# Staging the per-tile score-bound pass and the attention-value matmuls inside the head loop of a sparse-offset attention stage

## What is computed

```python
src = jnp.clip(t_idx[:, None] - offsets[None, :], 0, None)
Kg = k[:, :, src, :]
Vg = v[:, :, src, :]
scores = jnp.einsum('bhnd,bhnod->bhno', q, Kg) * scale
scores = scores + pos_bias.T[None, :, None, :]
scores = jnp.where(invalid[None, None], -jnp.inf, scores)
alpha = jax.nn.softmax(scores, axis=-1)
out = jnp.einsum('bhno,bhnod->bhnd', alpha, Vg)
gate = jax.nn.sigmoid(xn @ w_gate + b_gate)
x = x + out * gate @ w_out
```

## Time and profile before

| | us |
|---|---|
| median of two runs | 5897.9 |
| the profiled execution | 5880.33 |
| its span, slowest of 8 cores | 5878.7 |
| spans of the eight cores | 5846.4 to 5878.7 |
| PE busy | 4105.7 (70%) |
| DVE busy | 974.8 (17%) |
| ACT busy | 573.7 (10%) |
| exp, line 608, 256 times | 262.1 |
| mask multiply, line 611, 256 times | 177.2 |

### The profile page before, as it was taken

One profiled execution on the slowest core, in us unless ns is written; L12 is line 12 of the kernel. 1 busy time (PEld: TensorE's weight loads), 2 busy tenths in 40 slices (PEclk: granted clock), 3 DMA queues, 4 the chain that ended last, 5 costly groups with the idle time before them and its releaser, 6 DMA issues.

```text
span 5878.7 us, 54400 instructions; the slowest of 8 cores (5846.4 to 5878.7 us)
## 1 busy us (share of the span) xinstructions
PE 4105.7 (70%) x21474; PEld 2041.9 (35%) x21778; DVE 974.8 (17%) x1764; ACT 573.7 (10%) x546; POOL 194.4 (3%) x159
## 2 busy tenths in 40 slices
PE   0111777244444444454877898999999898999999
PEld 0000323233333333321433343444444443444444
DVE  0344224122222222234011111000000020000001
ACT  0000010111111111100200020000000100000000
POOL 0000000000000000000000010000000010000000
PEclk9655889555555555556988999999999999999999
DMA  3322121100000000023022366655656656555657
GB/s 57 83 57 57 29 71 26 30 12 12 6 12 7 10 12 6 12 60 93 19 40 61 118 76 83 82 72 73 83 75 103 119 72 88 77 72 78 80 72 136
DMA packets 493787, 342.64 MB, mean 58 GB/s; under 512 B 64563, under 2 KB 455732, under 8 KB 491492
## 3 DMA queue, kind: packets, MB, share of 16 engines
q0 software_dynamic: 384176, 219.69, 28.1%
q1 hardware_dynamic: 109364, 119.46, 7.4%
HBM read 513.56 MB, written 53.61 MB: 96 GB/s over the span
## 4 chain that ended last, share of the span: by engine, by line
PE 67%; DMA 11%; DVE 8%; ACT 5%; issue 4%; SPq 3%; DVEq 0%; ACTq 0%; POOLq 0%
PE p L900 40%; ACT s_E L608 4%; PE p_B L600 4%; PE p_B L591 4%; DVE s_at L611 3%; PE p_f L803 3%; PE p_A L621 3%; PE p_f L834 3%; PE p_f L784 3%; PE p_gm L400 2%; DMA s_xb<-xT 2%; PE p_gm L462 2%; PE p_o L714 1%; DVE s_b L562 1%; DMA s_hs<-h1T 1%
## 5 line engine op out<-in xcount | busy, mean ns | idle before, releaser
L900 PE MATMUL p<-s_hb,s_hs 128*128 128x512 bf16 x6021 | 1327.6, 380 | 50.2 <-DMA s_hs<-w1T 20.2
L900 PE MATMUL p<-s_ha,s_hs 128*128 128x512 bf16 x5018 | 1103.4, 380 | 44.3 <-DMA s_hs<-h1T 36.2
L900 PEld LDWEIGHTS p<-s_hb,s_hs 128*128 128x128 bf16 x6144 | 600.1, 98 | 777.7 <-issue 64.5
L900 PEld LDWEIGHTS p<-s_ha,s_hs 128*128 128x128 bf16 x5120 | 501.4, 98 | 646.4 <-issue 45.1
L621 PE MATMUL p_A<-s_V,s_at 128*128 128x65 bf16 x2048 | 153.3, 240 | 561.6 <-DVE s_at L611 561.6
L608 ACT ACTIVATE s_E<-p_B 128x1024 bf16<-128x1024 f32 x256 | 262.1, 1024 | 1187.8 <-PE p_B L600 1187.8
L958 DVE SCALAR_TENSOR_TENSOR s_oo<-p,s_s,s_rr 128x1024 f32<-128x1024 f32 x16 | 20.5, 1284 | 1995.8 <-PE p L900 1891.1
L621 PEld LDWEIGHTS p_A<-s_V,s_at 128*128 128x128 bf16 x2048 | 119.4, 126 | 622.4 <-issue 622.4
L310 PE MATMUL p_s<-s_xb,s_onescb 128*1 128x512 bf16 x56 | 24.7, 619 | 405.9 <-DMA s_xb<-xT 405.9
L591 PE MATMUL p_B<-s_nb,s_onesb 1*128 1x128 bf16 x2048 | 263.0, 305 | 62.1 <-DMA s_nb<-d_nb 62.1
L611 DVE TENSOR_TENSOR s_at<-s_E,s_MT 128x1024 bf16<-128x1024 bf16 x256 | 177.2, 692 | 733.5 <-ACT s_E L608 733.5
(11 more groups left out here) (99 smaller groups left out, 1899.2 us busy)
## 6 DMA issues: line engine op xcount, KB each, us to landing
s_hs<-h1T POOLq DMA_DIRECT2D x32, 2048.0 KB, 15.5
s_hs<-h2T POOLq DMA_DIRECT2D x32, 2048.0 KB, 15.3
s_hs<-w1T POOLq DMA_DIRECT2D x32, 512.0 KB, 5.8
s_hs<-w2T POOLq DMA_DIRECT2D x32, 512.0 KB, 5.8
s_hs<-w3T POOLq DMA_DIRECT2D x8, 2048.0 KB, 18.8
s_x<-xT SPq DMA_DIRECT2D x7, 2048.0 KB, 17.0
...
```

Source lines behind the costliest of these rows:

```text
L900: T(lambda t, o2=o2, kc=kc, b=b, pp=pp, src3=src3, sl3=sl3, n_kc=n_kc: t.matmul(pp[:, b * 512:(b + 1) * 512], sl3[:, kc, o2 * 128:(o2 + 1) ...
```

## The change

The body of the tile loop is split into functions: `p2_tile_loads`, `p2_passA_grp`, `p2_passA_tail`, `p2_passB` (score matmuls, exp, mask multiply of one head) and `p2_av` (AV, reciprocal, scaling of one head). They are called in another order: the loads and pass A of tile t+1 among the heads of tile t, and AV of head h-1 after the score matmuls of head h.

```diff
+    p2_tile_loads(0)
+    for grp in range(4):
+        p2_passA_grp(0, grp)
+    p2_passA_tail(0)
+    for qt in range(QT_N):
+        bi = qt & 1
         for h in range(H):
...
+            p2_passB(qt, h)
+            if qt + 1 < QT_N:
+                if h == 0:
+                    p2_tile_loads(qt + 1)
+                elif 1 <= h <= 4:
+                    p2_passA_grp(qt + 1, h - 1)
+                elif h == 5:
+                    p2_passA_tail(qt + 1)
+            if h >= 1:
+                p2_av(qt, h - 1)
+        p2_av(qt, H - 1)
```

s_b, s_nb, s_nbT, s_nb4, d_nb and the queue qNB get a second buffer by tile, s_E and s_at a second one by the parity of h. AV no longer writes p_A; it writes the first 65 columns of p_B of its head's parity, and p_B is free only after the scaling that reads them:

```diff
+    def p2_av(qt, h):
...
+            T(lambda t, jj=jj, ktile=ktile, h=h, pB=pB, par=par: t.matmul(
+                pB[:, 0:65],
+                s_at[par][:, jj * 128:(jj + 1) * 128],
...
+        V(lambda v, pB=pB: v.reciprocal(s_rd[:, :], pB[:, 64:65]),
...
+        st_p2["pB_free"][par] = vC.n
```

The score matmuls now wait for that, for s_nb4 and, in head 0 only, for the table and for q:

```diff
-            fw = [(vC, pB_free[par]), (qNB, nb4_q), (qMT, mt_q)]
+        fw = [(vC, st_p2["pB_free"][par]), (qNB[bi], st_p2["nb4"][bi])] +              ([(qMT, mt_q), (qQT[bi], st_p2["qld"][bi])] if h == 0 else [])
```

More of the change, by code:

```diff
@@ L84, in build_nc @@
 def build_nc(offsets, tap=None, upto=99, p2sub=99):
-    if p2sub < 99:
-        upto = 2
     offs = sorted(int(o) for o in np.asarray(offsets).tolist())
@@ L150, in build_nc @@
     d_grep = nc.dram_tensor("d_grep", [H, 128, GL], BF16, kind="Internal")
-    d_nb = nc.dram_tensor("d_nb", [H, 128], BF16, kind="Internal")
+    d_nb = nc.dram_tensor("d_nb", [2, H, 128], BF16, kind="Internal")
     P = Prog()
@@ L494, in build_nc @@
     qGD = [DS("qGD0"), DS("qGD1")]
-    qNB = DS("qNB")
+    qNB = [DS("qNB0"), DS("qNB1")]
     st2 = ExitStack()
@@ L511, in build_nc @@
     s_gd = [sb("s_gd0", [128, D], BF16, st2), sb("s_gd1", [128, D], BF16, st2)]
[L512 to L517, removed]
+    s_b = [sb("s_b0", [128, 16], F32, st2), sb("s_b1", [128, 16], F32, st2)]
+    s_nb = [sb("s_nb0", [128, 16], BF16, st2), sb("s_nb1", [128, 16], BF16, st2)]
+    s_nbT = [sb("s_nbT0", [16, 128], BF16, st2), sb("s_nbT1", [16, 128], BF16, st2)]
+    s_nb4 = [sb("s_nb40", [65, H * 128], BF16, st2), sb("s_nb41", [65, H * 128], BF16, st2)]
+    s_E = [sb("s_E0", [128, NJ * 128], BF16, st2), sb("s_E1", [128, NJ * 128], BF16, st2)]
+    s_at = [sb("s_at0", [128, NJ * 128], BF16, st2), sb("s_at1", [128, NJ * 128], BF16, st2)]
     s_rd = sb("s_rd", [128, 1], F32, st2)
@@ L521, in build_nc, with p2_tile_loads @@
     p_B = [ps("p_B0", [128, NJ * 128], F32, st2), ps("p_B1", [128, NJ * 128], F32, st2)]
-    p_av = p_A
     bstride = 1 - J[0]
[L525 to L531, removed]
+    st_p2 = {
+        "pB_free": [0, 0],
+        "mask_done": [0, 0],
+        "av_done_t": [0, 0],
+        "at_ms": {},
+        "pb_ms": {},
+        "qld": [0, 0],
+        "gld": [0, 0],
+        "nb4": [0, 0],
+        "gd_store": [0, 0],
+        "pA_guard": 0,
+        "trb_guard": 0,
+    }
+    def p2_tile_loads(qt):
         bi = qt & 1
@@ L536, in build_nc, with p2_passA_grp @@
            waits=[(tM, tM.n)])
-        qld = qQT[bi].n
+        st_p2["qld"][bi] = qQT[bi].n
         DA(qGT[bi], lambda s, qt=qt, bi=bi: s.dma_start(s_gtt[bi][:, :], d_gate.ap()[qt]),
            waits=[(vC, vC.n)])
-        gld = qGT[bi].n
+        st_p2["gld"][bi] = qGT[bi].n
+    def p2_passA_grp(qt, grp):
+        bi = qt & 1
         q3 = s_qt[bi][:, :].rearrange("p (c t) -> p c t", c=8)
-        if p2sub < 1:
-            continue
         t0col = HALO + qt * 128
[L546 to L566, removed]
@@ L567, in build_nc @@
-        if p2sub < 2:
-            continue
-        V(lambda v: v.tensor_scalar_mul(s_nb[:, :], s_b[:, :], -1.0))
+        start_col = t0col + 128 - bstride * 128
+        for hh in range(4):
+            h = grp * 4 + hh
+            g, r0 = h // 2, (h % 2) * 64
+            par2 = h % 2
+            fw = []
+            if hh == 0:
+                fw = [(vC, st_p2["pA_guard"]), (qQT[bi], st_p2["qld"][bi])]
+            T(lambda t, hh=hh, g=g, r0=r0, par2=par2, start_col=start_col, q3=q3: t.matmul(
+                p_A[par2][:, (hh // 2) * 128:(hh // 2 + 1) * 128],
+                q3[r0:r0 + 64, g, :],
+                K3[r0:r0 + 64, g, start_col:start_col + bstride * 128:bstride],
+                start=(hh < 2), stop=(hh >= 2),
+                tile_position=(r0, 0)),
+              incs=[(tM, 1)] if hh == 3 else (),
+              waits=fw if hh == 0 else ())
@@ new lines, in p2_passA_grp, with p2_passA_tail @@
+        amss = tM.n
+        for par2 in range(2):
+            V(lambda v, qt=qt, bi=bi, grp=grp, par2=par2: v.tensor_reduce(
+                s_b[bi][:, grp * 4 + par2: (grp + 1) * 4: 2],
+                p_A[par2][:, :].rearrange("p (h k) -> p h k", h=2),
+                axis=AX.X, op=ALU.max),
+              waits=[(tM, amss)] if par2 == 0 else ())
+        st_p2["pA_guard"] = vC.n
+    def p2_passA_tail(qt):
+        bi = qt & 1
+        V(lambda v, bi=bi: v.tensor_scalar_mul(s_nb[bi][:, :], s_b[bi][:, :], -1.0))
@@ L570, in build_nc @@
         nb_ms = vC.n
-        T(lambda t: t.transpose(p_trb[:, :], s_nb[:, :], s_id[:, :]),
-          incs=[(tM, 1)], waits=[(vC, nb_ms)])
+        T(lambda t, bi=bi: t.transpose(p_trb[:, :], s_nb[bi][:, :], s_id[:, :]),
+          incs=[(tM, 1)], waits=[(vC, nb_ms), (vC, st_p2["trb_guard"])])
         trb_ms = tM.n
-        V(lambda v: v.tensor_copy(s_nbT[:, :], p_trb[:, :]), waits=[(tM, trb_ms)])
+        V(lambda v, bi=bi: v.tensor_copy(s_nbT[bi][:, :], p_trb[:, :]), waits=[(tM, trb_ms)])
         nbT_ms = vC.n
-        DA(qNB, lambda s: s.dma_start(d_nb.ap(), s_nbT[:, :]), waits=[(vC, nbT_ms)])
@@ L577, in build_nc @@
[L577 to L584, removed]
-        for h in range(H):
-            par = h & 1
-            g, r0 = h // 2, (h % 2) * 64
-            pB = p_B[par]
-            fw = [(vC, pB_free[par]), (qNB, nb4_q), (qMT, mt_q)]
[L590 to L641, removed]
+        st_p2["trb_guard"] = nbT_ms
+        DA(qNB[bi], lambda s, bi=bi: s.dma_start(d_nb.ap()[bi], s_nbT[bi][:, :]),
+           waits=[(vC, nbT_ms)])
+        DA(qNB[bi], lambda s, bi=bi: s.dma_start(
+            bass.AP(s_nb4[bi], 0, [[64 * H * 128, 2], [128, H], [1, 128]]),
+            bass.AP(d_nb, bi * H * 128, [[0, 2], [128, H], [1, 128]])),
+           waits=[(qNB[bi], qNB[bi].n)])
@@ new lines, in p2_passA_tail, with p2_passB @@
+        st_p2["nb4"][bi] = qNB[bi].n
+    def p2_passB(qt, h):
+        bi = qt & 1
+        par = h & 1
+        g, r0 = h // 2, (h % 2) * 64
+        pB = p_B[par]
+        q3 = s_qt[bi][:, :].rearrange("p (c t) -> p c t", c=8)
+        fw = [(vC, st_p2["pB_free"][par]), (qNB[bi], st_p2["nb4"][bi])] +              ([(qMT, mt_q), (qQT[bi], st_p2["qld"][bi])] if h == 0 else [])
+        for jj in range(NJ):
+            T(lambda t, h=h, jj=jj, pB=pB, r0=r0, bi=bi: t.matmul(
+                pB[:, jj * 128:(jj + 1) * 128],
+                s_onesb[r0:r0 + 1, :],
+                s_nb4[bi][r0:r0 + 1, h * 128:(h + 1) * 128],
+                start=(jj % 4 == 0), stop=False,
+                tile_position=(r0, 0)),
+              waits=fw if jj == 0 else ())
+        for jj in range(NJ):
+            ktile = HT + qt + J[jj]
+            T(lambda t, jj=jj, ktile=ktile, g=g, r0=r0, pB=pB, q3=q3: t.matmul(
+                pB[:, jj * 128:(jj + 1) * 128],
+                K3[r0:r0 + 64, g, ktile * 128:(ktile + 1) * 128],
+                q3[r0:r0 + 64, g, :],
+                start=False, stop=(jj % 4 == 3),
+                tile_position=(r0, 0)),
+              incs=[(tM, 1)] if jj == NJ - 1 else ())
+        st_p2["pb_ms"][h] = tM.n
+        SE(lambda s, pB=pB, par=par: s.activation(s_E[par][:, :], pB[:, :], AF.Exp),
+           waits=[(tM, st_p2["pb_ms"][h]), (vC, st_p2["mask_done"][par])])
+        e_ms = sC.n
+        V(lambda v, h=h, par=par: v.tensor_tensor(
+            s_at[par][:, :], s_E[par][:, :], MT3[:, h, :], ALU.mult),
+          waits=[(sC, e_ms), (tM, st_p2["av_done_t"][par])])
+        st_p2["at_ms"][h] = vC.n
+        st_p2["mask_done"][par] = vC.n
@@ new lines, in p2_av @@
+    def p2_av(qt, h):
+        bi = qt & 1
+        par = h & 1
+        pB = p_B[par]
+        for jj in range(NJ):
+            ktile = HT + qt + J[jj]
+            T(lambda t, jj=jj, ktile=ktile, h=h, pB=pB, par=par: t.matmul(
+                pB[:, 0:65],
+                s_at[par][:, jj * 128:(jj + 1) * 128],
+                V4[:, ktile, h, :],
+                start=(jj == 0), stop=(jj == NJ - 1)),
+              incs=[(tM, 1)] if jj == NJ - 1 else (),
+              waits=[(vC, st_p2["at_ms"][h])] if jj == 0 else ())
+        av_ms = tM.n
+        st_p2["av_done_t"][par] = av_ms
+        V(lambda v, pB=pB: v.reciprocal(s_rd[:, :], pB[:, 64:65]),
+          waits=[(tM, av_ms)] +
+                ([(qGT[bi], st_p2["gld"][bi]), (qGD[bi], st_p2["gd_store"][bi])] if h == 0 else []))
+        V(lambda v, h=h, bi=bi, pB=pB: v.scalar_tensor_tensor(
+            s_gd[bi][:, h * 64:(h + 1) * 64], pB[:, 0:64], s_rd[:, :],
```

(12 more changed lines are left out.)

## The result

The changed kernel takes 5771.0 us (median of 11 runs, 5751.7 to 6182.7). Against the kernel before the ratio is 0.9743, 95% interval 0.969 to 0.9796: 2.6% faster, on 5897.9 us that is 152 us, with 120 to 183 as the interval. The profiled execution took 5771.0, its span is 5769.4 (core 3).

A forecast was written before the change was run, and what follows sets the result against it. The attention stage was taken as one serial chain per head, 4.71 us, plus 16.6 us of uncovered pass A per tile. Head loop -141 and clock -5 make -146 us: 5752 us against the median 5897.9, range 5705 to 5785.

The forecast's parts named there:

- the sum for the head loop: Attention stage: tiles of 82.5 us against 91.97 give -142.2 over fifteen, the last tile +1.3, together -141 us.
- the clock term: Attention stage: PE's clock may rise at each tile start, speeding one head's scores; taken as -5 us.
- The main step: Attention stage: pass A's 16.6 us between tiles go for 15 of 16 tiles; a head costs 5.00 us, 0.29 more.
- multiply to reciprocal: In each head on DVE: from mask multiply start to reciprocal start, multiply 0.69 plus step 0.17, together 0.86 us.
- scaling to scores: In each head: from the scaling's end on DVE to the score matmuls on PE, taken as 0.25 us.
- The upper ends of both steps: In each head: 0.17 us from multiply to reciprocal, 0.25 from scaling to scores, giving 5.00 us a head.
- the lower (0.10, 0.15): In each head: the same two steps at their cheaper values, giving 4.83 us a head.
- rival 1: Attention stage: the clock, once raised at a tile start, stays at 2.4 GHz; 246 us less, 5511 us; chance 0.05.
- dearer handovers (2): Head chain: each of three handovers costs 0.07 us more than taken; 48 us, giving 5800 us; chance 0.14.
- Full pipelining (3): Head loop: a head costs only its busiest engine, PE, 2.5 us; 560 us more saved, about 5100; chance 0.01.
- The slower case (4): Heads: ScalarE's exp read is held up by AV's PSUM access, 154 us more, 5906 us; chance 0.04.
- The q load: Issued after head 0's scores, it lands about 5.0 us after head 0's start, hidden; at worst 0.25 us shows.

The follow-up runs named there:

- e1: Changed kernel with AV back behind its own head's multiply, in its own PSUM buffers, pass A overlap kept; 5690.6 us, ratio 0.9634 to the kernel before.
- e2: Changed kernel with pass A back between the tiles, later AV kept; ratio 1.0067 to the kernel before, median 5987.8 us.
- e3: Changed kernel, same instruction order, but AV writes its own PSUM buffers, so scores need not wait for the scaling; ratio 0.8803 to the kernel before.
- e4: Changed kernel with reciprocal and scaling of h-1 ahead of the multiply of h on DVE; 5354.8 us, ratio 0.9066 to the kernel before.
- e8: Changed kernel without two of the four waits (table and q) ahead of head 0's score matmuls; measured once, 5749.7 us.
- e5: e3 reordered: q load before head 0, AV(15) after next tile's first scores, groups in heads 1, 3, 5, 7, transpose in head 10; 5125.9 us.
- e7: e5 with negated-maximum and score matmuls both reading 128 rows, their tile_position dropped; 4997.2 us, ratio 0.8452 to the kernel before.

## Why the prediction was right or wrong, term by term

- **The step that failed** is the sum for the head loop and the clock term beside it: -141 and -5 us were forecast, and the loop lost 128.5 on the profiled core and 129 on the average of the eight, with nothing for the clock. The mechanism was right. What was mis-sized is the tile, 82.5 us forecast and 83.2 measured in the mean, because the handovers of heads 0, 1 and 5 were priced with one or two waits where the edit has two and four. The terms follow.
- **The main step held**: pass A's 16.6 us go, and a head becomes dearer. A head was put at 5.00 and is 4.99, one with a group at 6.12 and is 6.11; multiply to reciprocal 0.86, scaling to scores 0.25 or 0.26. e1 and e2 show the two halves separately, e3 and e4 the link. The upper ends of both steps (0.17, 0.25) were right, the lower (0.10, 0.15) wrong: the step of the nearest instruction with the same list of waits gave the right figure.
- **The time**: 5752 forecast, 5771 measured, and the ratio puts it at 5746 on the 5897.9 us that the forecast started from. That 5746 lies so near is in part luck: the averages above and the head loop of the traces support a gain of about 130 us, not 152, and the forecast was 146. The mis-sized terms of a tile: head 5 was put at 6.09 and is 6.28, since negate to transpose took 0.27 and not 0.15 and AV came 0.19 and not 0.13 behind it; head 15 to 0 was put at 5.00 and is 5.20, since I counted two waits there and the edit has four (e8); the reciprocal of head 0, which stands in head 1, has four waits too, step 0.31 and not 0.17. These make 0.5 us a tile. Another 0.2 us is a head now and then that is 0.36 longer (5.35 for 4.99), which I did not count; such heads stand in the kernel before (5.06 for 4.71), in e1 and in e2 too, and their cause is open. Fifteen tiles make 11 us of this. Another 1 us is the tile before: 91.97 by its q loads, 91.89 by its exps.
- **The clock**: -5 was taken for a rise at each tile's start. It is zero: the stretch from 1774 to 1781, over such a start, reads 0.50. The ground for the term was weak, because the rise of the earlier trace rows came in matmuls of 128 rows, and e5 shows 0.50 with PE busy 98.36 of 100 us in this stage's mix. So rival 1 fails too, but the reason given against it (too little work between bursts) was not the whole one: in e5 matmuls of the same shapes, almost without a pause, stay at 0.50. The page TensorE: Matmul & The Clock Gate of the Trainium skill (Part 1: The HAM clock gate) says that sustained activity lifts the clock. The trace of e5 does not agree, with matmuls of one, 64 and 128 rows in turn; that of e7, where all but pass A's read 128, does, with 0.93. The measurement decides.
- **The rivals**: dearer handovers (2) are out for the plain heads, and are what heads 0, 1 and 5 show, at 0.5 us a tile and not the 3 of that rival. Full pipelining (3) did not come, for the reason given, but the remark that it could only be had with the scaling ahead of the multiply was too narrow: e3 has it with another buffer and DVE's order untouched. The slower case (4) is out, exp lasts 1024 ns beside AV (1751.83 and 1751.61). The q load was hidden as forecast: PE waited 16.5 us in 15 times for it, but the reduces of that head would have waited for the multiply anyway and start 0.17 behind it.
